# Grouping the probability-times-value products of an attention head group into two bursts

## The reference, cut to what matters

```python
att = einsum('bhqd,bhkd->bhqk', q, k) / sqrt(hd)      # 16 heads, hd = 16, T = 512
att = softmax(where(causal, att, -inf))
y = einsum('bhqk,bhkd->bhqd', att, v)                 # the product that is moved
```

## Time and profile before

| | |
|---|---|
| time, median of 3 runs | 2074.36 us (2073.33 to 2074.73) |
| span of the profiled execution | 2071.1 us |
| share of the span: PE, PEld, DVE, ACT, POOL | 90%, 54%, 57%, 47%, 44% |

### The profile page before, as it was taken

How to read it: one execution, slowest core, us unless ns; L and a number is a source line. 1 busy time by engine, 2 the same in 40 slices (tenths; PEclk the granted TensorE clock), 3 DMA queues, 4 the chain that set the end, 5 groups by cost and what they waited for, 6 DMA issues and landing times.

```text
span 2071.1 us, 47593 instructions
## 1 busy us (share of the span) xinstructions
PE 1863.6 (90%) x13586; PEld 1113.8 (54%) x13587; DVE 1182.3 (57%) x2533; ACT 975.3 (47%) x1577; POOL 913.7 (44%) x1585
## 2 busy tenths in 40 slices
PE   2699999999999999995799998849999999999996
PEld 2355555555555555543566665526555555555554
DVE  4577777777777777774357776713333333333332
ACT  1277777777677777773333224413333333333332
POOL 2133333333333333342201666755655565555564
PEclk9799999999999999996899999979999999999998
DMA  1212222222211222210546732213333333333332
GB/s 51 72 54 73 70 72 70 71 61 71 70 57 55 71 70 71 61 54 31 189 127 180 207 85 69 64 34 54 51 53 51 53 51 53 51 53 52 49 53 41
DMA packets 155387, 146.23 MB, mean 71 GB/s; under 512 B 32753, under 2 KB 145905, under 8 KB 155250
## 3 DMA queue, kind: packets, MB, share of 16 engines
q1 hardware_dynamic: 125042, 108.65, 17.3%
q0 software_dynamic: 30208, 35.81, 10.8%
HBM read 75.65 MB, written 43.52 MB: 58 GB/s over the span
## 4 chain that ended last, share of the span: by engine, by line
PE 41%; issue 24%; POOL 18%; DVE 5%; SPq 5%; DMA 3%; POOLq 3%; ACT 1%; DVEq 0%; ACTq 0%
PE bank L1470 12%; PE bank L1600 8%; PE bank L1531 6%; POOL xrow L724 6%; PE bank L1575 5%; POOL ga_col L720 5%; POOL tok_d L699 3%; PE bank L1636 3%; SPq L414 3%; PE bank L1547 2%; DMA tok_d<-tw_col,to_col 2%; SPq L410 1%; PE bank L1562 1%; POOL ad_col L732 1%; PE bank L1616 1%
## 5 line engine op out<-in xcount | busy, mean ns | idle before, releaser
L807 ACT ACTIVATE prob<-bank,exp_scale 128x512 f32<-128x512 f32 x640 | 429.1, 686 | 193.2 <-PE bank L1575 186.9
L619 POOL TENSOR_SCALAR_AFFINE_SELECT prob<-prob 128x256 f32<-128x256 f32 (+1 forms) x640 | 236.7, 374 | 486.0 <-ACT prob L807 485.0
L1071 DVE TENSOR_REDUCE mx<-bank 128x1 f32<-128x512 f32 (+2 forms) x768 | 361.5, 506 | 120.3 <-PE bank L1547 119.8
L1363 DVE TENSOR_TENSOR htl<-bank,hth 128x512 f16<-128x512 f32 x200 | 138.0, 690 | 436.1 <-ACT hth L895 430.5
L1470 PE MATMUL bank<-wbuf,xt 128*128 x1632 | 375.9, 380 | 0.6 <-DVE xt L1358 0.6
L741 POOL DMA_INDIRECT out_x<-ysb,ad_col x136 | 217.6, 1600 | 170.2 <-ACT ysb L931 149.3
L931 ACT ACTIVATE ysb<-bank,row_w 128x256 f32<-128x256 f32 x136 | 64.4, 473 | 460.4 <-DMA out_x<-ysb,ad_col 436.4
L1531 PE MATMUL bank<-k_op,q_op 96*128 96x512 f16 (+3 forms) x1024 | 251.1, 307 | 30.2 <-DVE mx L1080 12.4
L1575 PE MATMUL bank<-q_op,k_op 128*128 128x512 f16 (+3 forms) x1024 | 243.6, 299 | 12.3 <-ACT prob L807 11.4
L1470 PEld LDWEIGHTS bank<-wbuf,xt 128*128 128x128 f16 x1632 | 159.9, 98 | 164.0 <-issue 2.7
L1470 PE MATMUL bank<-wbuf,hth 128*128 x1088 | 189.5, 275 | 3.9 <-DVE htl L1363 3.1
(11 more groups left out here) (206 smaller groups left out, 2923.4 us busy)
## 6 DMA issues: line engine op xcount, KB each, us to landing
x_in<-in_L_attn_x SPq DMA_DIRECT2D x16, 512.0 KB, 4.4
q_op<-qkh SPq DMA_DIRECT2D x256, 32.0 KB, 1.9
k_op<-qkh SPq DMA_DIRECT2D x512, 16.0 KB, 1.8
xres<-in_L_attn_x SPq DMA_DIRECT2D x16, 512.0 KB, 4.7
x_d<-x SPq DMA_DIRECT2D x32, 256.0 KB, 2.1
xhl_d<-xhl SPq DMA_DIRECT2D x32, 256.0 KB, 2.4
xrow<-xhl_d SPq DMA_DIRECT2D x64, 128.0 KB
wbuf<-xhl_d SPq DMA_DIRECT2D x16, 512.0 KB, 4.7
```

The costliest lines, as they stand in the source:

```text
L619: nc.gpsimd.affine_select(out=v, in_=v, compare_op=ALU.is_ge, fill=0.0, base=0, pattern=pat, channel_multiplier=-1).then_inc(S["sel_done"], 1)
L807: nc.scalar.activation(prob[:, half, u, :], ps_t[u % 2][:], ACT.Exp, scale=exp_scale[:]).then_inc(S["exp_done"], 1)
L1071: return nc.vector.tensor_reduce(out, src[:, lo:lo + n], AX_X, ALU.max)
```

## The change

The table moves piece 0 (512 columns) from step 2 to step 4, where it stands directly ahead of piece 1 (384 columns), and piece 2 (128 columns) from step 5 to step 6, directly ahead of piece 3 (256 columns). The loop that issues the pieces is written so that a step can hold more than one. No instruction is added or removed, and no other engine's program changes.

```diff
-        MIX, O_OUT = (2, 4, 5, 6), 7
+        MIX, O_OUT = (4, 4, 6, 6), 7
...
-                        if has2 and s in MIX:
-                            mix(G - 2, (g - 2) % 4, par if g >= 2 else 1 - par, b if g >= 2 else b - 1,
-                                MIX.index(s))
+                        for piece in range(NT):
+                            if has2 and s == MIX[piece]:
+                                mix(G - 2, (g - 2) % 4, par if g >= 2 else 1 - par, b if g >= 2 else b - 1, piece)
```

## The result

The changed kernel takes 2099.26 us (median of 4 runs, 2098.18 to 2099.81), the one before 2073.89 us (4 runs). The ratio is 1.0118, 95% interval 1.0106 to 1.0131: 25.4 us slower.

A forecast was written before the change was run, and what follows sets the result against it. PE was taken to bound the attention. Group changes of +0.68, +0.59, +0.35 and +0.06 us, joins included, summed to 25.6 us; 2071.1 us span plus 25.6 and 3.3, less 0.6, gave 2099.4 us, 8-in-10 range 2083 to 2120.

The forecast's parts named there:

- What bounds: Attention, batches 1 to 14: PE bounds, a matmul under way 733.1 of 765.0 us; the pattern repeats within 0.01 us.
- The join: Two pieces back to back on PE: each join saves 0.21 us, two a group 0.42 us, 128 joins 27 us.
- the seam: Between two joined pieces: 0.03 us taken off the 0.24 us fixed part, leaving 0.21 us saved a join.
- Leaving step 2: Piece 0 taken from step 2 uncovers the copy on ACT; with joins, groups change +0.68, +0.59, +0.35, +0.06 us.
- Won of the 1.10 us: Part of piece 0's 1.10 us really gained at steps 2 and 3: groups 0 to 3, 0.00, 0.09, 0.33, 0.62 us.
- The total: Whole kernel: 2071.1 us span plus 25.6, median 3.3 above, 0.6 off for small idle stretches: 2099.4 us, +1.2%.
- Joins save nothing: Rival, both bursts: second piece's loads exposed or switch paid again, +53 us, half of it +39; chance 0.10.
- Fewer switches win: Rival: PE need not stand for the copy, so the joins' 27 us would be all, 2047 us; chance 0.04.
- Exposed weight loads: At a join: loads taking all 128 rows would not overlap running matmuls, so the second piece's are exposed; sum unchanged.
- Idle repaid: Rival: waits of steps 8 to 1 close, 2.3 us a batch back, 2068 us; 0.07 faster, 0.15 repaid in part.
- The signs: Expected in the profile: some 50 us of new PE waits in 64 groups, step 2 shorter by 1.1 us, gapless bursts.
- one sign of being wrong: Step 3: PE starting `shifted` of unit 0 over 0.1 us after the copy would mean something else binds.

The follow-up runs named there:

- e1: The kernel before with only pieces 2 and 3 joined at step 6, piece 0 kept at step 2 (2, 4, 6, 6): 2060.96 us, ratio 0.9942.
- e3: The kernel before with pieces 0 and 1 joined at step 2, pieces 2 and 3 at step 6 (2, 2, 6, 6): 2066.46 us, ratio 0.9966.
- e4: The kernel before with pieces 1, 2 and 3 in one burst at step 5 (2, 5, 5, 5): 2062.12 us, ratio 0.9945.
- e5: The kernel before with pieces 1, 2 and 3 in one burst at step 4 (2, 4, 4, 4): 2071.87 us, ratio 0.9976.

## Why the prediction was right, step by step

**What bounds.** Right: PE in the attention, and PE's waits with little slack. Outside the attention, before the first and after the last `scores`, the spans differ by 1.1 and 0.4 us. One premise was wrong: the pattern does not repeat from batch to batch to within 0.01 us. Before the change the 14 batches last 53.6 to 56.6 us. Group 1 repeats to 0.05 us, but group 3 has about 16 instead of 14.2 us in batches 4, 6, 8 and 10, where the program's loop turns, and group 0 after it varies from 11.3 to 12.8 us.

**The join.** Right in mechanism, taken a little low: 0.21 us chosen between 0 and 0.24, and 0.24 measured (steps 5 and 6 of group 1; the burst of three pays the fixed part once too). The 0.03 us taken off for the seam is not there: the pass behind the seam starts 0.42 us after the one ahead of it, no more than its 512 columns take.

**Leaving step 2.** Right, group by group. Won of the 1.10 us: in group 0 nothing (steps 2 and 3 together 3.07 before, 3.08 after), and the reading of why holds in nine of the 14 batches: DVE's line 977 ends and the transposes start 0.06 us later (0.15 in three of the nine). The PE and DVE timelines of the changed kernel, group 0 of batch 8:

```profile
520.15 0.39 PE L1531 MATMUL bank<-k_op,q_op 96*128 96x512 f16 x1 [0.28 <-DVE mx L1071]
...
520.84 0.39 PE L1575 MATMUL bank<-q_op,k_op 128*128 128x512 f16 x1 [0.23 <-ACT q_op L827]
521.35 0.66 PE L1461 MATMUL bank<-ident,xn 128*128 128x128 f32 x4
```

```profile
520.62 0.68 DVE L977 TENSOR_TENSOR xl<-bank,xh 128x512 fp32r<-128x512 f32 x1
```

In batch 1 and after the loop turns (5, 7, 9, 11) they start 0.5 to 0.7 us after line 977 and 0.2 to 0.3 us after `shifted`, which waited for the copy: there the copy binds in group 0 too. Group 0 changes by +1.02, +1.70, -0.19 and +1.72 us in the latter four, which the medians do not show.

In group 1 the copy and the exponential behind it bind; in group 2 the copy (steps 2 and 3 together 0.32 us shorter, 0.33 forecast); in group 3 line 1092 (0.61 us shorter, 0.62 forecast). Changes of a group, forecast and measured: +0.68 and +0.71; +0.59 and +0.56; +0.35 and +0.26; +0.06 and +0.01; a batch 1.68 and 1.54 by these medians, 1.67 by the length of the 14 batches, which has the loop turns in it. Two terms besides are off by more than 0.05 us: step 7 of group 0 is 0.07 us longer, where nothing was put, and step 5 of group 2 is 0.06 us shorter than a piece of 128 columns explains. In step 5 of group 2 `transpose_y` followed piece 2 directly; whether the piece costs more ahead of a float32 transpose was not tried.

**The total.** 2099.4 us forecast, 2099.26 measured. That is closer than the method is, and the last microseconds are luck. The sum put 25.6 less 0.6, 25.0 us, on the profiled span, and the span grew by 26.5. It then added 3.3 us from the span to the median, but each execution of the changed kernel is 1.7 us longer than its own span; the 3.3 set a span against the median of several executions. The 1.5 us too few and the 1.6 us too many cancel. In the attention too, errors cancel in part: the join was off by 0.03 x 128 = 4 us, and the groups at the loop turns went about 2.5 us the other way, group 0 after them by 2.0 and group 3 ahead of them by 0.5. These last come from one trace of each kernel.

**The rivals.** *Joins save nothing*: e1 rules it out, 2060.96 us where 2074 would have been the time. *Fewer switches win*: the joins do save 0.48 us a group, as the Trainium skill's rule on changing the tiling mode (TensorEngine Tiling (Array Packing), Tiling Modes) would have it, but PE stands for the copy. That the fixed part is a switch of the tiling mode, and not something else at the edge of a piece, no run here tells apart. *Exposed weight loads*: the trace of the changed kernel shows the second piece's loads, which take all 128 rows, under the running pass; the rule of the Trainium skill (TensorE: Matmul & The Clock Gate, Part 3), read strictly, does not hold here, and the measurement decides. The same Part of that page of the Trainium skill also lets loads into a background weight buffer run ahead; whether these are such loads no run here shows. *Idle repaid*: steps 8 to 1 last as long as before by the medians of all four groups, and 0.17 us a batch longer on average, at the loop turns; none came back.

**The signs.** Not all came as written. Some 50 us of waits were forecast for 64 groups, 47 for the 56 of the 14 batches; the idle time grew by 30.2. At least part of the difference is one of counting: in group 1 `shifted` starts 0.90 us after the mask product of its step, where 0.06 us is usual (532.93 to 532.99 in the rows of group 1), so PE stands 0.84 us where the view has 0.68. Step 2 was to be shorter by 1.1 us, which only groups 1 and 2 show nearly (1.09 and 0.97); in groups 0 and 3 part of the wait falls into step 2 itself (0.64 and 0.61). And one sign of being wrong was met: in ten of the 14 batches `shifted` of group 0 starts 0.13 us after the copy, over the 0.1 us that was set. In the batch shown it is 0.14, from 519.69 + 1.01 = 520.70 to 520.84. Where line 977 binds behind it, as here, it costs nothing; what takes the time is open.

```profile
519.69 1.01 ACT L827 ACTIVATE q_op<-bank 4x1024 f16<-4x1024 f32 x1 [0.77 <-PE bank L1562]
```

**What it missed** is outside the forecast itself: I held bunching to be free beyond the copy. It is nearly so for (4, 4, 6, 6), where group 0's step 7 has 0.07 us of new idle, but not for other placements. In e3 and e4 the burst that leaves step 4 uncovers what stood behind it (line 1092 in group 3), and in e5 three bare steps in a row outrun DVE in group 0.

## What to carry to other kernels

Work of the bound engine that stands between two ends of another engine's round trip is not free to move: before moving it, subtract the end of the releaser from the start of the waiting instruction, for each instance of the pattern, and go on to the next instruction in case it has less slack still. A saving that comes from joining short side-by-side products is real, and can be had by joining those pieces that cover nothing. Which pieces those are differs from group to group here, since each step covers something else in each of them.

## What the runs showed of the hardware

A piece of four float32 products of 32 output rows each, side by side in the array, costs 1.68 ns a column and 0.24 us besides (read from pieces of 128 to 384 columns); two or three such pieces back to back pay the 0.24 us once, even with a satisfied wait on each piece, and their weight loads hide under the pass before. PE starts 0.05 to 0.06 us after ACT or DVE ends in many of the open waits: all 28 for the copy in groups 1 and 2 of the changed kernel, all 14 of line 1624 in e4. It is not a constant: 0.13 us after the copy in ten of 14 batches of group 0, and 0.15 us in nine of 14 waits of `transpose_o` for line 1092 in group 3. Why, no run here tells. The new waits, 0.5 to 0.7 us in groups 1 and 2 and 0.9 at most, hardly moved the granted clock, the level of 2.4 GHz: 0.99 over the 14 batches, 1.00 before.
